# Attention maxima: one group of four heads in four PSUM banks in place of two groups of two heads

## The chip, the cores and the metric

The kernel runs on one core of one Trainium2 chip. The metric is the time of one execution on the device in microseconds; the time of a kernel is the median of several runs.

## The reference

The input is x (8192 tokens of 128 channels) and a dense 8192 x 8192 matrix adj. A graph layer comes first, then a transformer layer with experts:

```python
x = x + relu(A_norm @ (layernorm(x) @ W.T))     # A_norm: adj + I, scaled by row degrees
h = rmsnorm(layernorm(x)) ; q, k, v = rotated projections     # 4 heads of 32, 2 key heads
scores = where(causal, q @ k.T / sqrt(32), -1e30)
att = softmax(scores)                            # subtracts each row's maximum
y = x' + (att @ v) @ wo.T
out = y + sum over the 2 best of 8 experts of share * (silu(y2 @ w1.T) * (y2 @ w3.T)) @ w2.T
```

The change concerns the maximum of each row of scores, which the softmax needs for each of 4 heads and 8192 queries over all earlier keys.

## The kernel before, in words

The program has three stages, one after another: the graph stage (until about 1450 us of the profile), the attention stage (until about 3260 us) and the expert stage. Only the attention stage is touched.

Queries are taken in 16 blocks T of 512, each in two halves H of 256, so there are 32 halves; half 2T is the even one of its block, half 2T+1 the odd one. A half goes over the key blocks G = T, 0, 1, ..., T-1, in pairs of two subtiles of 128 keys. A pair is the step of the stage's loop; there are 528, with q as their number.

For each step TensorE makes the transposed scores of the next step in four products into a ring of three PSUM banks (L1450, `scores`), ScalarE takes their exponentials into `probs` (L1072), TensorE weighs the values with them (L1465, `weigh`), and sums the weights for the denominators, partly itself (L1474, `add_weights`) and partly on GpSimd (L978). A shift of each row, the row's maximum rounded to f16, is multiplied in as one more row of `q_stack`, so the maxima of a half must be known before its first scores.

The maxima come from a separate product with the upper halves of q and k alone: TensorE multiplies 128 queries of each head by up to 512 keys into `ps_max` (four PSUM banks, one for each head, L1431; on the diagonal block a mask is added by a product with the identity, L1436), and VectorE reduces it to one maximum for each query and head (L1202, `reduce_piece`). The work for one set of heads is a piece. `pieces` lists them by half, key block, subtile and group of heads; in an even half the diagonal piece holds both of its subtiles. HEADS is the heads in a piece, MAX_BUFFERS = NH // HEADS the pieces that `ps_max` holds at once; a fill waits until the piece MAX_BUFFERS before it is reduced (L1425).

The maxima of a half are taken while the half before is worked on. The pieces of a half are spread evenly over the steps between the starts of their two windows (`pieces_at`, L699 to L705): of the pieces of a step, the first AT_ONCE go into slot 0, between the two pairs of score products of the next step, the others into slot 1, after the sums of weights. At the end of its window VectorE takes the maximum over the key blocks (L1211, `find_shift`), one step later TensorE turns it (L1443, `turn_max`), ScalarE rounds it (L1088), and a DMA puts it into `q_stack`.

Each engine's order is written out by hand in program order; engines meet by semaphores. On VectorE a step's reduces come first, then `find_shift`, the reciprocals of the denominators (L1217) and the steps of the routing to experts. SP issues the loads, GpSimd the scatters of rows to the experts. The order of TensorE in a step is:

```python
scores_of(q + 1, lambda: find_maxima(q, 0))   # two products, slot 0, two products
for i in range(2): weigh(q, i)
add_weights(q)
find_maxima(q, 1)                             # slot 1
# then turn_max, combine, project, ... where they are due
```

Of the kernel before, what the change touches and what calls it, by code (L numbers as in the profile page):

```python
# [631 lines left out]
def attention_stage(nc, NB, dram, keep):  # L632
# [11 lines left out]
    QBUF = 3  # L644
    KEPT = 2
    RING = 3
    HEADS = 2
    MAX_BUFFERS = NH // HEADS
    AT_ONCE = 2
    SLOTS = 4  # L650
    FILL_ROWS = 8
    FILLED = P * FILL_ROWS * SUB
# [35 lines left out]
    for half in range(HALVES):  # L688
        T, H = divmod(half, 2)
        subtiles = (2 * H, 2 * H + 1)  # L690
        for unit in range(T + 1):
            for group in ([subtiles] if unit == 0 and H == 0 else [(s,) for s in subtiles]):
                for pair in range(NH // HEADS):
                    pieces.append((half, unit, group, pair))
# [6 lines left out]
    for half in range(2, HALVES):  # L701
        start, end, total = max(turned_at[half - 1], 0), turned_at[half], len(pieces_of[half])
        for q in range(start, end):
            here = pieces_of[half][(q - start) * total // (end - start):(q + 1 - start) * total // (end - start)]
            pieces_at[q, 0], pieces_at[q, 1] = here[:AT_ONCE], here[AT_ONCE:]  # L705

# [90 lines left out]
    with ExitStack() as ctx:  # L797
# [390 lines left out]
        def _(dve):  # L1188
# [4 lines left out]
            def reduce_piece(m):  # L1193
                half, unit, group, pair = pieces[m]
                heads, base = slice(pair * HEADS, (pair + 1) * HEADS), m % MAX_BUFFERS * HEADS
                dve.wait_ge(max_filled, m + 1)
# [3 lines left out]
                for s in group:  # L1200
                    width = (s + 1) * P if unit == 0 else BT
                    nc.vector.tensor_reduce(unit_max[:, half % 2, heads, s % 2, unit], ps_max[:, base:base + HEADS, at:at + width],  # L1202
                                            AX_X, ALU.max).then_inc(max_read, 1)
# [202 lines left out]
        def _(pe):  # L1406
# [9 lines left out]
            def max_piece(m):  # L1416
                half, unit, group, pair = pieces[m]
                T = half // 2
                G, diagonal, base = units_of(T)[unit], unit == 0, m % MAX_BUFFERS * HEADS
                if m == pieces_of[half][0]:  # L1420
# [6 lines left out]
                for s in group:  # L1427
                    width = (s + 1) * P if diagonal else BT
                    for n in range(HEADS):
                        rows = slice((pair * HEADS + n) * HD, (pair * HEADS + n + 1) * HD)  # L1430
# [522 lines left out]
def program(nc, N, dram):  # L1953
    NB = N // BT
    for name, shape, dt in (("x1", (NB, P, SUB, C), F32), ("z", (NB, P, SUB, C), F32),
                            ("lower", (NB, P, BT), F32), ("q_hi", (P, N), F16), ("q_lo", (P, N), F16), ("k_hi", (P, N), F16),
                            ("slots", (NE * N + GROUP, ROW), F32), ("parts0", (TOPK * N, C), F32),
                            ("parts1", (TOPK * N, C), F32)):
        dram[name] = nc.dram_tensor(f"scratch_{name}", shape, dt, kind="Internal").ap()
    with ExitStack() as ctx:  # L1960
        own = lambda stack, shapes: {name: stack.enter_context(nc.sbuf_tensor(f"keep_{name}", shape, dt))
                                     for name, shape, dt in shapes}
        keep = own(ctx, (("ident", [P, P], F32), ("ident16", [P, P], BF16),
                         ("mask_ts", [P, P], BF16), ("mask_st", [P, P], BF16), ("ones_heads", [P, HD], F32),
                         ("attended", [P, N], F32), ("rows", [P, 1, SUB, TOPK, ROW], F32),
                         ("slot_index", [P, 4 * SUB, TOPK], mybir.dt.uint32), ("taken", [P, NE], F32)))
        with ExitStack() as until_attended:
            keep |= own(until_attended, (("shared", [P, N + N // P * NKV * HD], F32),))
            keep["k_stack"] = keep["shared"][:, 0:N].bitcast(F16).rearrange("p (k n) -> p k n", k=NKV)
            keep["v"] = keep["shared"][:, N:].rearrange("p (n c) -> p n c", c=NKV * HD)  # L1970
            graph_stage(nc, NB, dram, keep)
            attention_stage(nc, NB, dram, keep)
        expert_stage(nc, NB, dram, keep)
# [56 lines left out]
```

## Time and profile before

| | us |
|---|---|
| median of 3 runs | 3701.52 |
| lowest, highest | 3696.71, 3705.01 |
| the profiled execution's own time | 3697.04 |
| its span in the profile | 3695.3 |

Mean granted TensorE clock over the span: 0.925. Times in the rows are counted from the span's start. PE is TensorE's products, PEld its weight loads, DVE VectorE, ACT ScalarE, POOL GpSimd. A product's end is modelled, while its weight load shows when it was issued; so the steps of TensorE are read from the weight loads. PEclk is the share of full clock granted in a stretch: 1.00 is 2.4 GHz, 0.50 is 1.2 GHz.

### The profile page before, as it was taken

How to read it: one execution, taken by the hardware profiler on the slowest of the kernel's cores; microseconds unless marked ns; L12 is line 12 of the kernel's file. 1: busy time of each engine (PE TensorE's matmuls, PEld its weight loads, DVE VectorE, ACT ScalarE, POOL GpSimd, SP SyncE). 2: the span in 40 equal slices, each digit the busy share in tenths (PEclk: the TensorE clock that was granted, in tenths of full speed). 3: DMA queues.
4: the chain of work that ended last, by engine and by line, in shares of the span. 5: the costliest groups of instructions: out<-in, count | busy, mean ns of one | idle time of the engine just before them, and what ended most of it. 6: DMA issues, size and time to landing. Idle time of an engine off the chain costs nothing. (4 is left out here: it accounts for less than half of the span.)

```text
span 3695.3 us, 56800 instructions
## 1 busy us (share of the span) xinstructions
PE 3115.2 (84%) x22369; PEld 1368.1 (37%) x22369; DVE 2580.5 (70%) x2752; ACT 1424.4 (39%) x2843; POOL 1690.7 (46%) x1094
## 2 busy tenths in 40 slices
PE   2578898999677884999999999999999999839990
PEld 1334443444333342343333333333333333315650
DVE  8888786773343443778878987877987898326773
ACT  0000000000000001565666666666666666735660
POOL 0000000002111111566788688877689778744653
PEclk9778999999888996999999999999999999969995
DMA  9898777676555762542221000000000000012226
GB/s 378 351 398 354 318 318 289 251 305 226 213 221 212 278 252 74 201 147 79 92 91 61 13 15 22 13 7 7 7 18 17 10 4 16 11 53 66 75 64 230
DMA packets 170238, 531.94 MB, mean 144 GB/s; under 512 B 20721, under 2 KB 66554, under 8 KB 125062
## 3 DMA queue, kind: packets, MB, share of 16 engines
q1 hardware_dynamic: 123752, 473.35, 33.3%
q10 hardware_dynamic: 33024, 31.47, 2.6%
q0 software_dynamic: 13200, 23.50, 2.0%
q8 instruction: 180, 2.95, 0.3%
q14 instruction: 82, 0.67, 0.1%
HBM read 434.70 MB, written 92.15 MB: 143 GB/s over the span
## 5 line engine op out<-in xcount | busy, mean ns | idle before, releaser
L1202 DVE TENSOR_REDUCE unit_max<-ps_max 128x2 f32<-128x1024 f32 (+2 forms) x1088 | 1226.1, 1171 | 310.5 <-PE ps_max L1431 265.6
L978 POOL TENSOR_TENSOR chunk_sum<-chunk_sum,probs 128x1024 f32<-128x1024 f32 x480 | 1132.2, 2359 | 307.9 <-ACT probs L1072 297.8
L1072 ACT ACTIVATE probs<-ps_ring 128x512 f32<-128x512 f32 x2112 | 1089.8, 595 | 437.1 <-PE ps_ring L1450 403.1
L537 PE MATMUL ps_gather<-ring,keep_attended 128*128 128x512 f32 x1688 | 803.1, 633 | 138.3 <-DMA ring<-in_adj 115.1
L1450 PE MATMUL ps_ring<-q_stack,keep_shared 97*128 97x512 f16 x2112 | 673.4, 385 | 27.8 <-ACT probs L1072 22.1
L1465 PE MATMUL ps_acc<-probs,keep_shared 128*32 128x256 f32 (+1 forms) x8448 | 565.6, 386 | 0.0
L537 PEld LDWEIGHTS ps_gather<-ring,keep_attended 128*128 128x128 f32 x1688 | 338.2, 205 | 548.4 <-issue 548.4
L352 DVE TENSOR_TENSOR work<-work,ring 128x2048 f32<-128x2048 f32 x195 | 446.7, 2291 | 38.8 <-DMA ring<-in_adj 35.0
L322 POOL DMA_DIRECT2D scratch_lower<-lower x13 | 7.3, 559 | 803.7 <-ACT lower L460 803.7
L1431 PE MATMUL ps_max<-k_heads,q_heads 32*128 32x512 f16 (+3 forms) x2176 | 277.0, 379 | 74.9 <-DVE unit_max L1202 48.2
L1474 PE MATMUL ps_acc<-probs,keep_ones_heads 128*32 128x256 f32 (+1 forms) x4224 | 326.9, 378 | 0.0
L1450 PEld LDWEIGHTS ps_ring<-q_stack,keep_shared 97*128 97x128 f16 x2112 | 163.5, 98 | 407.2 <-ACT probs L1072 254.0
L1465 PEld LDWEIGHTS ps_acc<-probs,keep_shared 128*32 128x32 f32 x8448 | 222.1, 110 | 244.7 <-issue 120.6
L1733 POOL DMA_INDIRECT scratch_parts<-moe_y_rows,moe_y_index x156 | 162.7, 1043 | 136.4 <-DMA scratch_parts<-moe_y_rows,moe_y_index 60.7
L330 POOL TENSOR_TENSOR q_lo<-rotated,q_hi 128x512 f16<-128x512 f32 x16 | 18.4, 1150 | 444.0 <-DVEq L436 444.0
L1431 PEld LDWEIGHTS ps_max<-k_heads,q_heads 32*128 32x128 f16 x2176 | 73.3, 91 | 344.3 <-DVE unit_max L1202 196.1
L1474 PEld LDWEIGHTS ps_acc<-probs,keep_ones_heads 128*32 128x32 f32 x4224 | 137.9, 111 | 86.9 <-issue 2.7
L537 PE MATMUL ps_gather<-keep_shared,keep_attended 128*128 128x512 f32 x360 | 161.2, 604 | 2.5 <-DVE keep_attended L361 2.5
L352 DVE TENSOR_TENSOR work<-work,keep_shared 128x2048 f32<-128x2048 f32 x45 | 103.1, 2292 | 79.7 <-DMA keep_shared<-in_adj 79.1
L517 PE MATMUL ps_turn<-keep_ident,normed 128*128 128x128 f32 x128 | 24.6, 325 | 150.6 <-DVE normed L424 120.1
L1016 POOL DMA_INDIRECT scratch_slots<-batch_rows,keep_slot_index x120 | 118.8, 990 | 44.9 <-POOL chunk_sum L978 25.0
L490 ACT ACTIVATE std<-var 128x4 f32<-128x4 f32 x32 | 6.6, 206 | 338.7 <-DVE var L80 338.7
(239 smaller groups left out, 2742.3 us busy)
## 6 DMA issues: line engine op xcount, KB each, us to landing
ring<-in_adj SPq DMA_DIRECT2D x302, 1024.0 KB, 14.1
keep_shared<-in_adj SPq DMA_DIRECT2D x45, 1024.0 KB, 10.2
scratch_slots<-empty_rows SPq DMA_DIRECT2D x16, 2080.0 KB, 14.1
scratch_parts<-empty_part SPq DMA_DIRECT2D x8, 2048.0 KB, 13.3
moe_parts<-scratch_parts SPq DMA_DIRECT2D x64, 256.0 KB, 4.5
moe_x_rows<-scratch_slots SPq DMA_DIRECT2D x39, 260.0 KB, 2.7
x_in<-in_x SPq DMA_DIRECT2D x16, 256.0 KB, 13.2
x_in<-in_x ACTq DMA_DIRECT2D x16, 256.0 KB, 4.1
```

The lines of the kernel that those rows point to most:

```text
L352: add = nc.vector.tensor_tensor(total, total, tile_of[g, False], ALU.add)
L517: last = nc.tensor.transpose(ps_turn[:, s * P:(s + 1) * P], tile(s), ident[:])
L537: last = nc.tensor.matmul(bank[:], support[:, s * SUB + c, :], tile_of[g, is_again][:, c * BT:(c + 1) * BT], start=(first and c == 0), sto ...
L978: steps.then(nc.gpsimd.tensor_tensor(totals, totals, weights, ALU.add))
L1016: pool.indirect_dma_start(dram["slots"], bass.IndirectOffsetOnAxis(slot_index[:, at, k:k + 1], 0), rows_of(b)[:, at // SUB, at % SUB, k, : ...
L1072: nc.scalar.activation(probs[:, q % SLOTS, i, kv, :, lo:], halves(bank)[:, :, lo:], ACT.Exp, scale=SCALE).then_inc(ring_read, 1)
L1202: nc.vector.tensor_reduce(unit_max[:, half % 2, heads, s % 2, unit], ps_max[:, base:base + HEADS, at:at + width], AX_X, ALU.max).then_inc( ...
L1431: last = nc.tensor.matmul(ps_max[:, base + n, at:at + width], q_heads[rows, T % 2, s * P:(s + 1) * P], k_heads[rows, G * BT:G * BT + width ...
L1450: last = nc.tensor.matmul(out[:, :, lo:], k_stack[0:STACK, kv, G * BT + j * P:G * BT + (j + 1) * P], q_stack[:, T % QBUF, H, kv * NREP:(kv ...
L1465: nc.tensor.matmul(ps_acc[h * HD:(h + 1) * HD, lo:HALF], values[:, G * SUB + j, kv * HD:(kv + 1) * HD], probs[:, q % SLOTS, i, kv, h % NRE ...
L1474: last = nc.tensor.matmul(ps_acc[at * HD:(at + 1) * HD, HALF + lo:], keep["ones_heads"][:], probs[:, q % SLOTS, i, 1, r, lo:], start=False ...
L1733: pool.indirect_dma_start(dram[f"parts{s % CHAINS}"], bass.IndirectOffsetOnAxis(y_index[:, g % 2, s:s + 1], 0), y_rows[:, g % 2, s, :], No ...
```

## The change

One group of four heads fills all four banks of `ps_max`, and one maximum instruction goes over 2048 columns. MAX_BUFFERS becomes 1, so a fill waits for the reduce of the piece right before it. AT_ONCE becomes 1, so slot 0 of a step holds one piece and a second one goes into slot 1. The products and their number stay the same.

```diff
     RING = 3
-    HEADS = 2
+    HEADS = 4
     MAX_BUFFERS = NH // HEADS
-    AT_ONCE = 2
+    AT_ONCE = 1
     SLOTS = 4
```

## Rows read from the trace of the kernel before

**Rows 1.** The page: busy time of each engine, share of the span, instructions.

```profile
PE 3115.2 (84%) x22369; PEld 1368.1 (37%) x22369; DVE 2580.5 (70%) x2752; ACT 1424.4 (39%) x2843; POOL 1690.7 (46%) x1094
```

**Rows 2.** Table of stretches: window, length, busy us of each engine, PEclk, DMA.

```profile
2400.00:2600.00 200.00, 196.00 (x2093) 76.31 (x2089) 158.52 (x149) 133.52 (x264) 150.23 (x71) 1.00 0.02 7
```

**Rows 3.** Timeline, an ordinary step: start, length, engine, idle before it and releaser.

```profile
2469.88 0.10 PEld L1431 LDWEIGHTS ps_max<-k_heads,q_heads 32*128 32x128 f16 x4 [0.42 <-DVE unit_max L1202]
...
2472.79 0.10 PEld L1431 LDWEIGHTS ps_max<-k_heads,q_heads 32*128 32x128 f16 x4 [0.42 <-DVE unit_max L1202]
...
2470.31 2.36 DVE L1202 TENSOR_REDUCE unit_max<-ps_max 128x2 f32<-128x1024 f32 x2 [0.56 <-PE ps_max L1431]
```

**Rows 4.** Groups by shape, 1400 to 3000 us: count, busy us, mean ns, idle before.

```profile
L1202 DVE TENSOR_REDUCE unit_max<-ps_max 128x2 f32<-128x1024 f32 x894 | 1050.7, 1218 | 271.6 <-PE ps_max L1431 246.1 <-PE ps_max L1436 22.3
...
L1202 DVE TENSOR_REDUCE unit_max<-ps_max 128x2 f32<-128x256 f32 x32 | 13.4, 418 | 16.7 <-PE ps_max L1436 16.4
```

**Rows 5.** Timeline of VectorE, steps with a reciprocal.

```profile
2001.22 2.29 DVE L1202 TENSOR_REDUCE unit_max<-ps_max 128x2 f32<-128x1024 f32 x2
...
2003.42 0.94 DVE L1217 RECIPROCAL denominators<-denominators 128x128 f32<-128x128 f32 x1
...
2004.28 2.29 DVE L1202 TENSOR_REDUCE unit_max<-ps_max 128x2 f32<-128x1024 f32 x2
```

**Rows 6.** Timeline, four reduces in a row and the fill that waits.

```profile
1470.27 4.62 DVE L1202 TENSOR_REDUCE unit_max<-ps_max 128x2 f32<-128x1024 f32 x4 [3.08 <-PE ps_max L1431]
1471.55 0.10 PEld L1431 LDWEIGHTS ps_max<-k_heads,q_heads 32*128 32x128 f16 x2 [1.82 <-DVE unit_max L1202]
```

**Rows 7.** All that touches ps_max: what VectorE idled for, us and times.

```profile
  PE ps_max L1431: 265.6, 312
```

**Rows 8.** Timeline of weight loads, two steps in the middle of a half.

```profile
2472.25 0.11 PEld L1450 LDWEIGHTS ps_ring<-q_stack,keep_shared 97*128 97x128 f16 x2 [0.41 <-ACT probs L1072]
...
2475.49 0.11 PEld L1450 LDWEIGHTS ps_ring<-q_stack,keep_shared 97*128 97x128 f16 x2 [0.23 <-issue]
...
2476.88 0.09 PEld L1431 LDWEIGHTS ps_max<-k_heads,q_heads 32*128 32x128 f16 x2 [0.76 <-DVE unit_max L1202]
...
2479.17 0.11 PEld L1450 LDWEIGHTS ps_ring<-q_stack,keep_shared 97*128 97x128 f16 x2 [0.41 <-ACT probs L1072]
```

**Rows 9.** Timeline of weight loads, three steps at an even half's end.

```profile
2508.32 0.11 PEld L1450 LDWEIGHTS ps_ring<-q_stack,keep_shared 97*128 97x128 f16 x2 [0.41 <-ACT probs L1072]
2508.86 0.10 PEld L1431 LDWEIGHTS ps_max<-k_heads,q_heads 32*128 32x128 f16 x4 [0.42 <-DVE unit_max L1202]
...
2511.23 0.09 PEld L1431 LDWEIGHTS ps_max<-k_heads,q_heads 32*128 32x128 f16 x2 [0.41 <-issue]
2511.55 0.11 PEld L1450 LDWEIGHTS ps_ring<-q_stack,keep_shared 97*128 97x128 f16 x2 [0.23 <-issue]
...
2512.95 0.09 PEld L1431 LDWEIGHTS ps_max<-k_heads,q_heads 32*128 32x128 f16 x2 [0.47 <-DVE unit_max L1202]
...
2518.88 0.11 PEld L1450 LDWEIGHTS ps_ring<-q_stack,keep_shared 97*128 97x128 f16 x2 [0.41 <-ACT probs L1072]
```

**Rows 10.** Timeline of weight loads, first and last of three steps, odd half's end.

```profile
2433.75 0.21 PEld L1450 LDWEIGHTS ps_ring<-q_stack,keep_shared 97*128 97x128 f16 x2
...
2444.16 0.11 PEld L1450 LDWEIGHTS ps_ring<-q_stack,keep_shared 97*128 97x128 f16 x2 [0.41 <-ACT probs L1072]
```

**Rows 11.** Weight loads around two waits, and the two stretches with PEclk.

```profile
2056.16 0.09 PEld L1431 LDWEIGHTS ps_max<-k_heads,q_heads 32*128 32x128 f16 x2 [1.04 <-DVE unit_max L1202]
...
2641.53 0.10 PEld L1431 LDWEIGHTS ps_max<-k_heads,q_heads 32*128 32x128 f16 x2 [1.04 <-DVE unit_max L1202]
...
2645.36 0.11 PEld L1450 LDWEIGHTS ps_ring<-q_stack,keep_shared 97*128 97x128 f16 x2 [0.42 <-issue]
...
2052.00:2058.00 6.00, 4.81 (x55) 1.82 (x58) 5.83 (x10) 3.42 (x7) 3.04 (x3) 1.00 0.01 3
2640.00:2646.00 6.00, 5.05 (x37) 1.54 (x36) 5.96 (x7) 2.30 (x5) 2.74 (x2) 0.72 0.01 3
```

## The prediction

> **What bounds the kernel now.** I read the page first, then a table of stretches, then the timeline of TensorE's weight loads, which shows when each product is issued. On the page TensorE is the busiest engine [rows 1]. In a stretch in the middle of attention TensorE is busy for 196 of 200 us and VectorE for 159 [rows 2]. So in this stage TensorE sets the time, and VectorE, which takes the maxima of later rows beside it, matters only where TensorE waits for it. Graph and expert stages are not touched.
>
> An ordinary step issues, in this order: two score products, the maxima products of slot 0, two score products, the weighting products, the sums of weights, the maxima products of slot 1. It takes 2.91 us from one maxima fill to the next [rows 3]. The fill of four heads is issued at 2469.88; VectorE starts reducing at 2470.31, 0.43 later, and is done with both pairs 2.36 later, at 2472.67; the next fill goes out at 2472.79 [rows 3]. VectorE's end and TensorE's wish meet within 0.12 us.
>
> **What the change does.** Before, there are two pieces (pairs of heads) for each thing to reduce and two buffers. By the schedule in the code 432 steps hold two pieces, and 60 hold more: mostly three, in the middle and at the end of each half. After, a piece is four heads and all four banks, and a fill waits for the reduce of the piece before. 460 steps hold one piece. The surplus step in the middle of a half is gone, and 32 steps hold two pieces or more, one of them at the end of each half. Five of the 32 lie in the first six steps; of the other 27 the last has no piece behind it, so 26 full ones count.
>
> **Ordinary steps: nothing, by cover.** The new instruction over 2048 columns is not in the trace. 256 columns took 418 ns and 1024 took 1218 [rows 4], so 1024 more add 1067 and give an estimate of 2.29 us. The bounds are 2.20 (two reduces back to back, from their start at 2001.22 to that of the next operation at 2003.42, [rows 5]) and 2.44 (twice 1218). From a reduce's end to the next fill passes 0.06: the first of four reduces from 1470.27 ends at 1471.49, and the fill it releases is issued at 1471.55 [rows 6]. The new loop is thus 0.43 + 2.29 + 0.06 = 2.78 us, and TensorE comes back after 2.91. The single buffer is hidden by 0.13 us of scores, weighting and sums. If that cover is gone, each of 460 steps pays what is missing.
>
> The Trainium skill (Perfetto Trace Analysis, section Matmuls) says that independent matmul groups should rotate through different PSUM banks, so that one's evacuation overlaps the next one's matmuls. It speaks against this change; taken at its word for each step, its sum is that of the third rival below. Rows 3 speak against it for ordinary steps, because there TensorE has 2.4 us of other work between two fills.
>
> **Steps that VectorE paces: -6 us.** Where a reciprocal stands between the reduces, a step takes 3.06 (2001.22 to 2004.28), and two reduces in it 2.29 together [rows 5], the same as the new single one. Elsewhere the pair takes 2.36. In all, VectorE waited for a fill 312 times [rows 7], in 528 steps, so at most 216 are paced by it. The gain per step is between 0 and 0.15 (2.44 less 2.29), 0 to 32 us in all; I take 0.03, nearest to the pairs, and 6 us. A reciprocal or a routing operation between two reduces costs nothing new, since TensorE refills while it runs.
>
> **The middle surplus step goes: -29 us.** In step 2472.25 the third pair is issued at its end and lengthens it to 3.24, 0.33 over 2.91. In the next, from 2475.49, the second pair waits 0.76 for VectorE, which is a reduce behind, and that step takes 3.68, 0.77 over [rows 8]. That is 1.1 for each half, and 27 halves have such a middle (the first five halves are counted below): 27 x 1.1 = 29 us. Bounds: 9 (0.33 each, where VectorE paces both neighbours) and 37 (some are followed by a fall of the clock).
>
> **The double step at the end of a half: +45 us.** Take the one at 2508.32 [rows 9]. Scores go out, and 0.54 later the first fill (2508.86). VectorE starts at 0.97 and ends at 3.26, so the second fill, in slot 1, goes out at 3.32, where in before the third pair went out at 2.91 (2511.23). A fill holds TensorE for 0.32 (2511.23 to 2511.55), four heads side by side as long as two. The next step therefore starts at 3.64 in place of 3.23: +0.41. Its own fill, a diagonal one, would go out 0.54 later, at 4.18. It must wait for the second reduce, which starts at 3.75 and ends at 6.04, so it goes out at 6.10. TensorE stands still for 1.92 us between the two halves of the scores. Queued behind it are the other scores, the weighting, the sums and the turn of the maxima; ScalarE waits for the scores and GpSimd for ScalarE.
>
> Against this the diagonal fills get shorter, because four heads run side by side where two pairs followed each other: 0.32 for each of the two diagonal steps after an even half, and 0.2 of the 0.47 that the second pair waited at 2512.95 [rows 9], together 0.8; 0.4 after an odd half, whose successor has one diagonal step. So an even end costs 0.41 + 1.92 - 0.8 = 1.53 on the 10.56 us from 2508.32 to 2518.88, and an odd one 1.93 on the 10.41 from 2433.75 to 2444.16 [rows 9, 10]. 13 of each are 45 us. Where VectorE paces, only the two refills of 0.49 count, 25 us in all.
>
> **The start: +3 us.** Before the loop, three fills each wait for one reduce, and in the first six steps there are six surplus pieces of four heads, where before there were twelve of two. Nine refills at 0.49 us would be 4 us, less what the surplus pieces of before waited; I take 3, with bounds of 0 and 10 (the refills at half the clock).
>
> **The clock: +23 us.** At 2641.53, after waits of TensorE on VectorE that ended with 1.04 us, the granted clock of the stretch is 0.72, so the 1.2 GHz level for part of it; around a wait of the same length at 2056.16 it stayed at 1.00, all 2.4 GHz [rows 11]. From the fill at 2641.53 to the next step's scores passed 3.83 us, against 2.37 for the same work in rows 9 (2508.86 to 2511.23): a fall costs 1.46. The new waits (0.41 and 1.92 within 3.2 us) are longer than the single waits of these two cases, where it fell once and held once. I take 16 falls in 26 ends, 23 us; bounds 0 and 38, or 76 if a fall lasts twice as long.
>
> **Sum.** -6 - 29 + 45 + 3 + 23 = +36 on the profiled execution's own 3697.04 us: 3733. That execution stands 4.5 below the median of the runs, so on the scale of the median it is 3737.
>
> **Rivals.** *The clock holds.* TensorE works before and after each wait, as around 2056.16, and there is no fall: +13, 3714. *The clock falls at each end, and for longer.* The Trainium skill (TensorE: Matmul & The Clock Gate, A second HAM failure mode) tells of kernels whose cycling through PSUM makes TensorE idle briefly and its clock go up and down; by it this rival is the likely one. Rows 11 show one fall and one hold at like waits. 26 x 1.46 to 2.92 give +51 to +89, 3752 to 3790.
>
> *The ordinary step slips.* If the new instruction and its two handoffs take over 2.91, because VectorE starts only behind the fourth head or the reduce is near its upper bound of 2.44, then 460 steps pay: 0.1 is +46 on top, 3783; with no cover at all 0.49 each, +225. For it speaks the margin of 0.13, against it that the margin before was smaller still [rows 3] and held.
>
> *Faster: VectorE paces, not TensorE.* Then the middle steps cost little today, the ends only their two refills (+25), and each of 528 instructions saved gives back up to 0.15: -79 + 25 + 3 = -51, 3650. It decides once some 190 steps or more give the full 0.15, since 25 + 3 = 28 us must be outweighed. The Trainium skill (VectorE: DVE Perf Modes, Rules for kernel authors) asks for a smaller count of operations, and on VectorE alone it would give this. Against it: two reduces without a wait cost 2.29 to 2.36, not 2.44, and TensorE was busy for 196 of 200 us [rows 2, 5].
>
> *No difference.* If 13 of the 45 us at the ends fall together with waits that are there anyway (for routing on VectorE, for GpSimd's sums) and the clock holds, nothing is left: 3701. For it speaks that most halves hold routing steps, against it that rows 9 and 10 show ends with nothing of that kind beside them.
>
> **Chances.** The forecast (3715 to 3752) 0.50; the clock holds 0.14; falls longer 0.13; the ordinary step slips 0.07; faster 0.08; no difference 0.08. The range from 3700 to 3775 leaves out the faster case, most of the slips and half of the long falls. 0.2% is 7.4 us, about what a measurement of this kernel can tell. Below 3694 lie the faster case and a little of the fifth (0.10), within 7.4 us of 3701.5 the rest of it and the low end of a held clock (0.13), above it 0.77.
>
> **What would show it.** Right: L1202 on 128x2048 near 2.29 us; ordinary steps still 2.91; no surplus in the middle of a half; at each end a wait of TensorE for L1202 near 1.9 us between two score fills, 26 of them, and one of 0.4 before; in some of these a clock below 1.00. Wrong: ordinary steps over 2.95, a reduce over 2.44, end waits under 1 us, or a total wait of TensorE on VectorE that went down.

## The result, and the profile after

The changed kernel takes 3731.12 us (median of 4 runs, 3728.17 to 3738.65) against 3699.12 for the kernel before (4 runs, 3696.71 to 3705.01; three of them are those of the table of before). The ratio is 1.0087, 95% interval 1.0066 to 1.0109: slower by 32 us. The profiled execution took 3728.29 us, its span is 3726.6, its mean granted clock 0.919.

These are lines of the page of the changed kernel (busy time of the engines; then the group of the maxima: count, busy us, mean ns, idle before it). The last line is the same group on the page of the kernel before.

```profile
PE 3082.0 (83%) x22369; PEld 1359.2 (36%) x22369; DVE 2552.8 (69%) x2208; ACT 1421.3 (38%) x2843; POOL 1685.1 (45%) x1094
...
L1202 DVE TENSOR_REDUCE unit_max<-ps_max 128x4 f32<-128x2048 f32 (+2 forms) x544 | 1192.1, 2194 | 374.3 <-PE ps_max L1431 302.4
...
L1202 DVE TENSOR_REDUCE unit_max<-ps_max 128x2 f32<-128x1024 f32 (+2 forms) x1088 | 1226.1, 1171 | 310.5 <-PE ps_max L1431 265.6
```

544 maximum instructions stand where there were 1088. VectorE's busy time fell by 28 us [rows 1], and the kernel became slower all the same. On the two pages the idle time of VectorE before a maximum rose from 310.5 to 374.3 us, and that of TensorE before the products of the fills (L1431) from 74.9 to 142.6: each waits longer for the other.

The timeline of VectorE in the changed kernel has the new instruction (start, length, engine, operation, idle before it) at the end of a half, and further on with a reciprocal between two.

```profile
2528.66 2.29 DVE L1202 TENSOR_REDUCE unit_max<-ps_max 128x4 f32<-128x2048 f32 x1 [0.62 <-PE ps_max L1431]
2531.57 2.29 DVE L1202 TENSOR_REDUCE unit_max<-ps_max 128x4 f32<-128x2048 f32 x1 [0.62 <-PE ps_max L1431]
2534.37 2.29 DVE L1202 TENSOR_REDUCE unit_max<-ps_max 128x4 f32<-128x2048 f32 x1 [0.51 <-PE ps_max L1431]
...
2566.01 2.23 DVE L1202 TENSOR_REDUCE unit_max<-ps_max 128x4 f32<-128x2048 f32 x1
2568.15 0.93 DVE L1217 RECIPROCAL denominators<-denominators 128x128 f32<-128x128 f32 x1
2569.01 2.23 DVE L1202 TENSOR_REDUCE unit_max<-ps_max 128x4 f32<-128x2048 f32 x1
```

The instruction takes 2.29 us. From 2528.66 to 2531.57 is an ordinary step, 2.91 as before [rows 3]. With a reciprocal a step takes 3.00 (2566.01 to 2569.01), where it took 3.06 [rows 5].

The next lines are the weight loads of TensorE in the changed kernel: the same three steps as rows 9, at the end of the same half; and the three steps at the end of an earlier even half.

```profile
2237.85 0.12 PEld L1450 LDWEIGHTS ps_ring<-q_stack,keep_shared 97*128 97x128 f16 x2 [0.41 <-ACT probs L1072]
...
2241.52 0.11 PEld L1450 LDWEIGHTS ps_ring<-q_stack,keep_shared 97*128 97x128 f16 x2 [0.23 <-issue]
2244.05 0.13 PEld L1431 LDWEIGHTS ps_max<-k_heads,q_heads 32*128 32x128 f16 x4 [2.42 <-issue]
...
2247.57 0.32 PEld L1450 LDWEIGHTS ps_ring<-q_stack,keep_shared 97*128 97x128 f16 x2
...
2251.29 0.11 PEld L1450 LDWEIGHTS ps_ring<-q_stack,keep_shared 97*128 97x128 f16 x2 [0.41 <-ACT probs L1072]
...
2530.58 0.12 PEld L1450 LDWEIGHTS ps_ring<-q_stack,keep_shared 97*128 97x128 f16 x2 [0.41 <-ACT probs L1072]
2531.12 0.10 PEld L1431 LDWEIGHTS ps_max<-k_heads,q_heads 32*128 32x128 f16 x4 [0.42 <-DVE unit_max L1202]
...
2533.92 0.10 PEld L1431 LDWEIGHTS ps_max<-k_heads,q_heads 32*128 32x128 f16 x4 [0.83 <-DVE unit_max L1202]
2534.25 0.11 PEld L1450 LDWEIGHTS ps_ring<-q_stack,keep_shared 97*128 97x128 f16 x2 [0.23 <-issue]
2536.78 0.13 PEld L1431 LDWEIGHTS ps_max<-k_heads,q_heads 32*128 32x128 f16 x4 [2.42 <-issue]
...
2539.28 0.21 PEld L1450 LDWEIGHTS ps_ring<-q_stack,keep_shared 97*128 97x128 f16 x2
...
2542.44 0.11 PEld L1450 LDWEIGHTS ps_ring<-q_stack,keep_shared 97*128 97x128 f16 x2 [0.41 <-ACT probs L1072]
```

Read the lower half first. The second fill of the doubled step goes out 3.34 us after the step's start (2533.92), and the diagonal fill 2.53 after the scores of the next step (2536.78), where 0.54 is the ordinary distance: a wait of 1.99. The row puts it down to "issue", with no releaser. VectorE's rows name it: the reduce from 2534.37 ends at 2536.66, and 0.12 later the fill goes out. The three steps take 11.86 us; before they took 10.56 [rows 9].

The upper half is the same code with the same wait (2241.52 to 2244.05, again 2.53), but the next step starts only at 2247.57, 3.52 after the fill, where the lower half needs 2.50. All three take 13.44. The table of stretches of the changed kernel (window, length, busy us of the engines, PEclk, DMA) says why:

```profile
2244.00:2248.00 4.00, 3.92 (x36) 1.67 (x37) 1.97 (x2) 1.11 (x3) 3.34 (x3) 0.68 0.07 21
2534.00:2540.00 6.00, 4.04 (x47) 1.57 (x47) 4.31 (x3) 2.53 (x6) 2.69 (x2) 1.00 0.01 3
2400.00:2600.00 200.00, 194.12 (x2113) 75.30 (x2101) 153.68 (x78) 133.85 (x266) 152.69 (x72) 1.00 0.02 7
```

After the wait that begins at 2241.52 the granted clock fell to its 1.2 GHz level for a part of the stretch (0.68); after the one that begins at 2534.25 it stayed at 2.4 GHz (1.00). Between 1515 and 3230 us the record of the granted clock has 18 stretches at 1.2 GHz, before it had 5. Of the 18, one stands in each of 15 half ends (the three steps as above), where before one end held one.

With the start of each step taken from its first score product, the two profiles can be set side by side, step by step (steps 1 to 525):

| steps | after less before, us |
|---|---|
| ends of the 27 halves from the sixth on, three steps each | +61.9 |
| middles of these halves, two steps each | -28.0 |
| steps 1 to 7 | +3.3 |
| all others | -1.4 |
| sum | +35.8 |

Step 1 began 2.5 us earlier in the profile of the changed kernel, and behind the loop 2 us more are gained; so the span grew by 31.3. These 4.5 us are not shown to come from the change: a second profile of the changed kernel (`changed_again`) agrees with the first over these steps within 0.2 us, and its span is 3.1 us shorter.

### The profile page after: what moved, and what is told of

Its sections match the earlier page's. It is cut to its first block and busy times, and to the rows that moved or that the text cites. A ratio compares the mean times of both kernels' runs of the same rounds, so it can differ in the third digit from the quotient of the medians.

```text
span 3726.6 us, 56256 instructions
## 1 busy us (share of the span) xinstructions
PE 3082.0 (83%) x22369; PEld 1359.2 (36%) x22369; DVE 2552.8 (69%) x2208; ACT 1421.3 (38%) x2843; POOL 1685.1 (45%) x1094
## 5 line engine op out<-in xcount | busy, mean ns | idle before, releaser
L1202 DVE TENSOR_REDUCE unit_max<-ps_max 128x4 f32<-128x2048 f32 (+2 forms) x544 | 1192.1, 2194 | 374.3 <-PE ps_max L1431 302.4
L1450 PE MATMUL ps_ring<-q_stack,keep_shared 97*128 97x512 f16 x2112 | 681.3, 388 | 28.2 <-ACT probs L1072 23.5
L1465 PE MATMUL ps_acc<-probs,keep_shared 128*32 128x256 f32 (+1 forms) x8448 | 576.4, 392 | 0.0
L352 DVE TENSOR_TENSOR work<-work,ring 128x2048 f32<-128x2048 f32 x195 | 446.6, 2290 | 35.8 <-DMA ring<-in_adj 32.0
L1431 PE MATMUL ps_max<-k_heads,q_heads 32*128 32x512 f16 (+3 forms) x2176 | 212.2, 380 | 142.6 <-DVE unit_max L1202 114.0
L1431 PEld LDWEIGHTS ps_max<-k_heads,q_heads 32*128 32x128 f16 x2176 | 55.9, 91 | 377.4 <-DVE unit_max L1202 231.2
```

Of the source, the lines that this page charges most:

```text
L352: add = nc.vector.tensor_tensor(total, total, tile_of[g, False], ALU.add)
L1431: last = nc.tensor.matmul(ps_max[:, base + n, at:at + width], q_heads[rows, T % 2, s * P:(s + 1) * P], k_heads[rows, G * BT:G * BT + width ...
L1450: last = nc.tensor.matmul(out[:, :, lo:], k_stack[0:STACK, kv, G * BT + j * P:G * BT + (j + 1) * P], q_stack[:, T % QBUF, H, kv * NREP:(kv ...
L1465: nc.tensor.matmul(ps_acc[h * HD:(h + 1) * HD, lo:HALF], values[:, G * SUB + j, kv * HD:(kv + 1) * HD], probs[:, q % SLOTS, i, kv, h % NRE ...
```

## The experiments

The theory: the loss sits in the doubled step at the end of a half, where two refills follow one another with too little other work of TensorE between them; part of it is the wait, part the fall of the clock behind it. Ordinary steps hide the single buffer. The rivals: the missing buffer costs at every piece; VectorE's count of instructions sets the pace; the clock falls because of short bursts and not because of the wait. Each kernel was timed beside the kernel before; falls of the clock are counted between 1515 and 3230 us.

**The doubled step moved.** Of the n + 1 pieces of a half's n steps, two go into the seventh step of the window, in which TensorE also makes the denominators (halves from 8 on).

```diff
+            sets = total
+            long = first_of[half - 1] + 2 - start
+            ends = [n * sets // (end - start) for n in range(end - start + 1)]
+            if half > 4 and long < end - start:
+                ends = [n + (n > long) for n in range(end - start + 1)]
-            here = pieces_of[half][(q - start) * total // (end - start):(q + 1 - start) * total // (end - start)]
+            here = pieces_of[half][ends[q - start]:ends[q + 1 - start]]
```

> The changed kernel with one edit: the step that takes two pieces is no longer the last of a half's window but the one in which TensorE also makes the denominators (a 4.53 us step before and after). Theory (the loss lies in the doubled step at the end of a half, because too little other TensorE work stands between its two refills): the second fill still waits 0.4 us, the next one only 0.3 us in place of 1.9, and the clock falls at the ends go away. 26 x 1.6 = 43 us and some 20 us of falls less than the changed kernel: about 3668 us (3655 to 3685), under both kernels. Rival (the missing second buffer costs at every piece, wherever the doubled step stands): no change from the changed kernel, 3725 to 3738.

Measured: 3671.22 us, ratio 0.9924 of before (0.9902 to 0.9947), against 1.0087 for the changed kernel; 4 falls of the clock. Weight loads of this kernel, around the doubled step:

```profile
2513.51 0.11 PEld L1455 LDWEIGHTS ps_ring<-q_stack,keep_shared 97*128 97x128 f16 x2 [0.41 <-ACT probs L1077]
2514.05 0.10 PEld L1436 LDWEIGHTS ps_max<-k_heads,q_heads 32*128 32x128 f16 x4 [0.42 <-DVE unit_max L1207]
...
2516.85 0.10 PEld L1436 LDWEIGHTS ps_max<-k_heads,q_heads 32*128 32x128 f16 x4 [0.83 <-DVE unit_max L1207]
2517.17 0.30 PEld L1493 LDWEIGHTS ps_ring<-parity_sums,even_and_odd 128*128 128x128 f32 x2 [0.23 <-issue]
...
2518.79 0.11 PEld L1455 LDWEIGHTS ps_ring<-q_stack,keep_shared 97*128 97x128 f16 x2 [0.41 <-issue]
2519.64 0.10 PEld L1436 LDWEIGHTS ps_max<-k_heads,q_heads 32*128 32x128 f16 x4 [0.74 <-DVE unit_max L1207]
```

The second fill again goes out 3.34 after the start. But the denominators (2517.17 to 2518.79) now stand between it and the next one, which is late by 0.31 only (0.85 after its scores, not 0.54). The step with the denominators takes 5.28 us, 4.53 before: the surplus costs 0.75 there. With the same single buffer, the same instruction and the same number of doubled steps the kernel is faster than before. The rival that charges every piece is out.

**Two buffers, same places.** Pairs of heads as before, placed two by two where the changed kernel places its fours.

```diff
-            here = pieces_of[half][(q - start) * total // (end - start):(q + 1 - start) * total // (end - start)]
+            sets = total // 2
+            here = pieces_of[half][(q - start) * sets // (end - start) * 2:(q + 1 - start) * sets // (end - start) * 2]
```

> Two double-buffered groups of two heads as before, but the pieces go into the steps of the changed kernel: no surplus in the middle of a half, four pairs in the last step. Theory: the middles give back their 28 us; at the ends the third and fourth pair wait 0 to 0.5 us and the two diagonal pairs together 0.5 to 1, so an end costs some 1.2 us more than before, with few falls of the clock: about 3705 us (3696 to 3718). Rival (what costs is the single buffer alone, at every piece): without it only the gain of the middles is left, about 3671 us.

Measured: 3708.09 us, ratio 1.0037 (1.0021 to 1.0052), 8 falls. Weight loads at the end of the half of rows 9:

```profile
2509.72 0.11 PEld L1451 LDWEIGHTS ps_ring<-q_stack,keep_shared 97*128 97x128 f16 x2 [0.41 <-ACT probs L1073]
...
2512.64 0.09 PEld L1432 LDWEIGHTS ps_max<-k_heads,q_heads 32*128 32x128 f16 x2 [0.41 <-issue]
2513.11 0.09 PEld L1432 LDWEIGHTS ps_max<-k_heads,q_heads 32*128 32x128 f16 x2 [0.37 <-DVE unit_max L1203]
2513.43 0.11 PEld L1451 LDWEIGHTS ps_ring<-q_stack,keep_shared 97*128 97x128 f16 x2 [0.23 <-issue]
2514.41 0.12 PEld L1432 LDWEIGHTS ps_max<-k_heads,q_heads 32*128 32x128 f16 x2 [0.87 <-issue]
...
2515.48 0.09 PEld L1432 LDWEIGHTS ps_max<-k_heads,q_heads 32*128 32x128 f16 x2 [0.66 <-DVE unit_max L1203]
```

The wait is there with two buffers too, in three smaller parts, because VectorE has four reduces to do in a row. The end costs 1.13 us over before (11.69 for the three steps) where the single buffer costs 1.30. Over all 27 ends it is 36.6 us with two buffers and 61.9 with one. So the doubled step by itself is most of the loss; the single buffer adds the longer unbroken wait, and with it more falls of the clock (18 against 8).

**Two buffers, doubled step moved.** The edit of the first experiment, on the kernel before.

```diff
+            sets = total // 2
...
-            here = pieces_of[half][(q - start) * total // (end - start):(q + 1 - start) * total // (end - start)]
+            here = pieces_of[half][ends[q - start] * 2:ends[q + 1 - start] * 2]
```

> Two double-buffered groups of two heads as before, with both surplus pairs in the step that also makes the denominators. Theory: middle steps minus 1.1 us, ends minus 0.3, this step plus 0.75: 26 x 0.67 = 17 us under before, about 3682 us (3672 to 3692). If placing does not matter: as before, 3699. Against the kernel with the same places and one group of four it tells what the two buffers are worth once the places are right: the theory expects them to be worth nothing, or less, because diagonal fills of four heads side by side are shorter by 0.3 to 0.6 us a half.

Measured: 3678.76 us, ratio 0.9955 (0.9935 to 0.9975), 4 falls. Once the doubled step is well placed, two buffers are worth nothing: 0.9924 with one group of four. The intervals overlap, so that the single group is the better one rests on the steps of the two profiles, which are 6.4 us shorter in sum with it: the diagonal step at the end of an even half mostly takes 3.01 us with one group and 3.38 with two.

**Two instructions for the maximum.** The changed kernel, with one edit:

```diff
-                    nc.vector.tensor_reduce(unit_max[:, half % 2, heads, s % 2, unit], ps_max[:, base:base + HEADS, at:at + width],
-                                            AX_X, ALU.max).then_inc(max_read, 1)
+                    for h in range(0, HEADS, 2):
+                        last = nc.vector.tensor_reduce(unit_max[:, half % 2, h:h + 2, s % 2, unit],
+                                                       ps_max[:, h:h + 2, at:at + width], AX_X, ALU.max)
+                    last.then_inc(max_read, 1)
```

> The changed kernel, with its maximum taken by two instructions over 1024 columns each, one wait in front and one signal behind. Theory: 2.36 us for the pair in place of 2.29; the ordinary step has 0.13 us to spare, so only the ends pay, three times 0.07: about 5 us over the changed kernel, 3736 us (3730 to 3742). Rival (VectorE sets the pace and the smaller count of instructions is what the change gained): up to 0.15 us for each of 528 pieces, 20 to 79 us over the changed kernel.

Measured: 3744.76 us, ratio 1.0132 (1.0106 to 1.0158), by the ratios 13 to 17 us over the changed kernel (1.0098 when it was timed again, 1.0087 the first time); the expectation of 5 was too low. Step by step the two profiles differ by 12.0 us; the ends alone give 13.7, the first seven steps -3.6, all others +1.8. An even end whose clock held costs 1.43, against 1.30; the rest goes with more falls (23 against 18). So the merging of instructions brings nothing in ordinary steps, and the rival by VectorE's count is out.

**Four instructions.** The same edit with one head each, shown against the kernel with two.

```diff
-                    for h in range(0, HEADS, 2):
-                        last = nc.vector.tensor_reduce(unit_max[:, half % 2, h:h + 2, s % 2, unit],
-                                                       ps_max[:, h:h + 2, at:at + width], AX_X, ALU.max)
+                    for h in range(HEADS):
+                        last = nc.vector.tensor_reduce(unit_max[:, half % 2, h:h + 1, s % 2, unit],
+                                                       ps_max[:, h:h + 1, at:at + width], AX_X, ALU.max)
```

> The changed kernel, with its maximum taken by four instructions over 512 columns, one wait in front and one signal behind. It measures the cover of the ordinary step: three joints of 0.07 make the reduces 2.50 in place of 2.29, and the loop of refill and reduce 2.99. Theory (0.13 us to spare in an ordinary step): some 390 ordinary steps grow by 0.07 to 0.08, 29 us; the ends by 26 x 3 x 0.2 = 16, and with a few more falls of the clock the whole is 45 to 60 us over the changed kernel, 1.021 to 1.025 of before. If the ordinary step has more to spare than that (0.2 or over): ends only, 16 to 30 us, 1.013 to 1.017.

> The changed kernel once more, on the same chip as the two others, so that they are compared on one chip: 1.0066 to 1.0109 of before, with 13 or more falls of the clock in the stretch of the maxima if they come from the waits at the ends.

Measured: four instructions 3782.81 us, ratio 1.0247 (1.0227 to 1.0266); the changed kernel on the same chip 3727.48, ratio 1.0098 (1.0078 to 1.0118). The difference is 55 us. Weight loads and VectorE of the kernel with four instructions, in ordinary steps:

```profile
2225.46 0.10 PEld L1433 LDWEIGHTS ps_max<-k_heads,q_heads 32*128 32x128 f16 x4 [0.58 <-DVE unit_max L1203]
...
2228.45 0.10 PEld L1433 LDWEIGHTS ps_max<-k_heads,q_heads 32*128 32x128 f16 x4 [0.58 <-DVE unit_max L1203]
...
2225.91 2.48 DVE L1203 TENSOR_REDUCE unit_max<-ps_max 128x1 f32<-128x512 f32 x4 [0.50 <-PE ps_max L1433]
2228.90 2.48 DVE L1203 TENSOR_REDUCE unit_max<-ps_max 128x1 f32<-128x512 f32 x4 [0.51 <-PE ps_max L1433]
```

2.48 of reducing and 0.51 for the refill are 2.99, and where such steps follow one another 2.99 is now the step. This shows the cover of the changed kernel's ordinary step: 2.29 + 0.51 = 2.80, so 0.11 us is spare, and a reduce longer by 0.19 overdraws it. It does so less often than expected. Of 211 steps that take 2.91 in the changed kernel (ends, middles and the start aside) 90 stay and some 90 grow by 0.06 to 0.08. All steps but the ends give 21 us, not 29; the ends give 29.6, with 109 us at 1.2 GHz in place of 72.

**A shorter last reduce.** In the changed kernel the maximum of each half's last piece goes over half of its columns; the maxima of the other keys of that piece are left out.

```diff
+                    read = width // 2 if half > 4 and m == pieces_of[half][-1] else width
-                    nc.vector.tensor_reduce(unit_max[:, half % 2, heads, s % 2, unit], ps_max[:, base:base + HEADS, at:at + width],
+                    nc.vector.tensor_reduce(unit_max[:, half % 2, heads, s % 2, unit], ps_max[:, base:base + HEADS, at:at + read],
                                             AX_X, ALU.max).then_inc(max_read, 1)
```

> The changed kernel, but the maximum of the last piece of each half is taken over the first half of its columns only (1024 in place of 2048; the maxima of those keys are left out). Every fill, wait and instruction stays. Theory (the wait at the ends is VectorE's reduce, and TensorE's clock falls because of it): the wait shrinks from 1.92 to 0.85 us, 26 x 1.07 = 28 us, and the falls of the clock at the ends, 14 to 18 in the changed kernel, mostly go, some 18 us: about 46 us under the changed kernel, near 0.996 of before. Rival (the clock falls because TensorE is fed in short bursts through one set of banks, whatever the length of the wait): 28 us only, near 1.001 of before, with 15 falls or more left.

Measured: 3682.55 us, ratio 0.9972 (0.9960 to 0.9985), 45 us under the changed kernel on the same chip; 6 falls of the clock in place of 18. VectorE and weight loads of this kernel at the end of the half of rows 9:

```profile
2499.66 1.23 DVE L1203 TENSOR_REDUCE unit_max<-ps_max 128x4 f32<-128x1024 f32 x1 [0.50 <-PE ps_max L1432]
...
2499.54 0.11 PEld L1451 LDWEIGHTS ps_ring<-q_stack,keep_shared 97*128 97x128 f16 x2 [0.23 <-issue]
2501.00 0.13 PEld L1432 LDWEIGHTS ps_max<-k_heads,q_heads 32*128 32x128 f16 x4 [1.35 <-issue]
```

From the scores to the diagonal fill pass 1.46 us, 1.07 less than 2.53, as the reduce is shorter by 1.06. Ends whose clock had held mostly got shorter by 1.07, and twelve of the fifteen others by 2.6 to 2.7: the difference of some 1.58 is the price of a fall. Three ends and three other places still have one. So most of the falls at the ends hang on the length of the wait, and the rival by short bursts is out for them; what the three that are left hang on is not shown. The Trainium skill (TensorE: Matmul & The Clock Gate, A second HAM failure mode) tells of a clock that goes up and down under cycling through PSUM. These runs agree that brief waits suffice (1.99 us at the ends), and show that a wait 1.07 us shorter in the same cycle is enough to prevent most falls.

## Why the prediction was right

The forecast was +36 us (3737 on the scale of the median, 3700 to 3775), by the case that had the highest chance; measured were 3731.12, +32 by the two medians and +31.3 in the profiles. The mechanism is the one forecast. That the sum came so near is in part luck: two terms missed by 5 to 6 us each in opposite directions (the steps paced by VectorE, and the ends with their falls), and the steps alone gave +35.8, with -4.5 us outside them.

- **Ordinary steps at nothing.** Right. The instruction takes 2.29 us as estimated, the step stays at 2.91. The spare time was taken as 0.13 and is 0.11: VectorE starts 0.45 after the fill (2531.12 to 2531.57), not 0.43. The experiment with four instructions shows that this is what stands between the changed kernel and a loss in many ordinary steps. The rule of the Trainium skill (Perfetto Trace Analysis, section Matmuls) on rotating through banks holds at the ends, where too little else covers the refill; in ordinary steps not following it cost nothing here.
- **Steps paced by VectorE, -6.** All other steps together gave -1.4; a reciprocal step 0.06 each. The sign was right, the size too large.
- **Middles, -29.** Measured -28.0.
- **The start, +3.** Measured +3.3 on steps 1 to 7. From the loop's first score product on it is 2.4; the three fills before the loop, which the term has too, can't be told from what varies in the stage ahead.
- **Ends, +45, and falls of the clock, +23.** Together 68; measured +61.9. By the price of a fall some 22 of them are falls (14 more ends with one, at 1.58) and some 40 the waits. The shape is the one worked out: second fill at 3.34 (3.32), diagonal fill at 6.20 (6.10), with the clock held three even ends at 1.30 (1.53) and two odd ones at 1.83 (1.93). By these numbers the diagonal steps of such an even end got shorter by 1.1, where 0.8 was allowed for. Some ends next to routing cost under 1 us, as the bound for steps paced by VectorE had it. Falls were taken in 16 ends at 1.46; they came in 15, at some 1.58. That part was a guess between bounds and fell well, which is luck: the profile before could not settle it.

What fell of the rivals: the slipping step, by rows of the profile after; a faster kernel by VectorE, by the two instructions; a clock that holds, by the 18 falls; a clock that falls at each end, by the 12 of 27 ends without one; no difference, by the 32 us.

## What to carry to other kernels

A single buffer is free where the consumer's time and both handoffs (here 2.29 + 0.51 us) fit between two refills (2.91), and it costs most where two refills meet with little else between; so look for the steps that hold one more than the others, not for the mean. Such a surplus belongs into the step that has the most other work on the waiting engine: moved there, one group of four heads went from 1.0087 of the time before to 0.9924, and without touching the buffers the kernel before went to 0.9955. A wait on TensorE can cost more than its length, since the clock may fall behind it.

## What was not expected of the hardware

The falls of the clock repeat: the changed kernel, profiled twice, fell 18 times in each, at the same steps, with starts 0.4 to 0.5 us apart, as its loop was (1470.5 and 1470.1 us for step 1). And ends of like code differ by it: the steps at 2241.52 and at 2534.25 hold the same wait of 1.99 us, after the same 0.42 before it, and the clock fell behind one and held behind the other. Why this one and not that one was not settled.
